# An AFNO block pair on one core: a tile's low half moved ahead of a Newton chain, and the next image's statistics one tile pair behind instead of two

## What is computed

```python
residual = x
h = layer_norm(x, n1_g, n1_b)
h = afno_filter(h, w1, b1, w2, b2)      # rfft2, block MLP with relu and softshrink, irfft2, + its input
h = h + residual
residual = h
h = layer_norm(h, n2_g, n2_b)
h = jax.nn.gelu(h @ mw1 + mb1, approximate=False)
h = h @ mw2 + mb2
return h + residual
```

## Time and profile before

| what | value |
|---|---|
| median of 3 runs | 1695.14 us (1693.17 to 1696.4) |
| the profiled execution, time | 1697.64 us |
| its span, first to last instruction | 1695.9 us |
| PE busy | 1611.5 us, 95% of the span |
| VectorE, ScalarE, GpSimd busy | 1136.1, 949.7, 628.3 us (67, 56, 37%) |
| mean granted clock of TensorE | 0.996 |

### The profile page before, as it was taken

One profiled execution on the slowest core, in us unless ns is written; L12 is line 12 of the kernel. 1 busy time (PEld: TensorE's weight loads), 2 busy tenths in 40 slices (PEclk: granted clock), 3 DMA queues, 4 the chain that ended last, 5 costly groups with the idle time before them and its releaser, 6 DMA issues.

```text
span 1695.9 us, 35295 instructions
## 1 busy us (share of the span) xinstructions
PE 1611.5 (95%) x11336; PEld 1458.9 (86%) x11336; DVE 1136.1 (67%) x2879; ACT 949.7 (56%) x1774; POOL 628.3 (37%) x792
## 2 busy tenths in 40 slices
PE   0799999999999999999999999999999999999999
PEld 0799978888999988888889998888889998788888
DVE  7979576666649856666666976666664795665563
ACT  3655366666535546666634644666663563666665
POOL 3900037776710005777760000777774000111111
PEclk9999999999999999999999999999999999999999
DMA  8400613333300062333320024333332006011111
GB/s 215 180 26 1 227 43 99 105 99 105 101 32 1 13 226 77 110 93 103 108 88 1 1 94 138 94 100 111 105 101 69 2 1 207 14 38 31 37 31 50
DMA packets 166369, 138.86 MB, mean 82 GB/s; under 512 B 9218, under 2 KB 129284, under 8 KB 166276
## 3 DMA queue, kind: packets, MB, share of 16 engines
q1 hardware_dynamic: 165988, 137.15, 25.4%
q10 hardware_dynamic: 288, 0.46, 0.1%
HBM read 70.47 MB, written 67.11 MB: 81 GB/s over the span
## 4 chain that ended last, share of the span: by engine, by line
PE 88%; DVE 4%; POOL 2%; ACT 2%; issue 1%; DMA 0%; DVEq 0%; ACTq 0%
PE ps L692 27%; PE ps L683 7%; PE ps L685 7%; PE ps L639 7%; PE ps L684 7%; PE ps L578 7%; PE ps L534 6%; PE ps L524 5%; PE ps L549 3%; PE ps L672 3%; PE ps L551 3%; PE ps L658 3%; PE ps L664 3%; POOL first L1273 1%; POOL xout L1269 1%; DVE stats L943 1%
## 5 line engine op out<-in xcount | busy, mean ns | idle before, releaser
L692 PEld LDWEIGHTS ps<-mw,gel 128*128 128x128 f32 x4096 | 533.2, 191 | 43.3
L692 PE MATMUL ps<-mw,gel 128*128 128x128 f32 x4096 | 536.4, 274 | 0.0
L803 ACT ACTIVATE gel<-ps,mb1f 128x512 f32<-128x512 f32 x512 | 351.7, 687 | 266.6 <-PE ps L685 235.6
L1314 POOL TENSOR_TENSOR arena<-arena,mb2rep 128x512 f32<-128x512 f32 x128 | 163.8, 1281 | 796.4 <-ACT hn L789 796.4
L683 PE MATMUL ps<-hth,mw1h 128*128 128x512 f32 x512 | 259.9, 508 | 7.5 <-DVE htl L1111 6.5
L1307 POOL TENSOR_SCALAR arena<-xnext,rstd,shift 128x128 f32<-128x128 f32 x384 | 168.8, 463 | 219.4 <-DVE shift L1238 219.4
L789 ACT ACTIVATE hn<-arena,shift,rstd 128x128 f32 (+1 forms) x512 | 221.5, 482 | 24.2 <-DVE shift L1238 23.9
L1094 DVE TENSOR_TENSOR arena<-ps,arena 128x512 f32 (+1 forms) x60 | 41.4, 691 | 259.6 <-PE ps L664 240.9
L685 PE MATMUL ps<-hth,mw1l 128*128 128x512 f32 x512 | 202.1, 395 | 0.0
L684 PE MATMUL ps<-htl,mw1h 128*128 128x512 f32 x512 | 200.9, 392 | 0.0
L774 ACT ACTIVATE osb<-usb,vectors 128x512 f32<-128x512 f32 (+1 forms) x136 | 95.7, 704 | 121.1 <-DVE usb L1002 121.1
(11 more groups left out here) (101 smaller groups left out, 2434.8 us busy)
## 6 DMA issues: line engine op xcount, KB each, us to landing
arena<-aside SPq DMA_DIRECT2D x128, 256.0 KB, 4.8
aside<-gz SPq DMA_DIRECT2D x96, 256.0 KB, 2.9
between<-xout SPq DMA_DIRECT2D x62, 256.0 KB, 2.3
xnext<-between SPq DMA_DIRECT2D x62, 256.0 KB, 3.0
out_dram<-xout SPq DMA_DIRECT2D x62, 256.0 KB, 2.3
aside<-first SPq DMA_DIRECT2D x32, 256.0 KB, 2.3
xnext<-in_x_dram SPq DMA_DIRECT2D x31, 256.0 KB, 3.0
mw1raw<-in_L_mw_dram SPq DMA_DIRECT2D x4, 256.0 KB, 2.5
```

The costliest lines, as they stand in the source:

```text
L692: mm = pe.matmul(ps[:, r % 2, P * i:P * i + P], gel[:, r % 2, m, P * i:P * i + P], mw2[:, m, :], start=(m == 0 and i == 0), stop=(m == CHU ...
L803: act.activation(gel[:, r % 2, m, :], ps[:, 2 + m % 2], ACT.Gelu, bias=mb1f[:, m:m + 1]).then_inc(gelu_out, 1)
L1314: pool.tensor_tensor(t, t, b, ALU.add).then_inc(mb2_done, 1)
```

## The change

Two things are changed, by code written in another order.

First, at the start of the MLP stage, the second tile: TensorE transposes it after the first chunk of `fc1` instead of the second, ScalarE casts it before gelu 1 instead of gelu 2, and VectorE forms its low half before the second Newton chain instead of behind it.

Second, from pair 4 on, pair q handles the next image's pair q - 1. To get there, an additional chain for the next image's pair 2 stands alone behind pair 3 (`nearer`), with a third set of statistics buffers, and only one chain is left behind pair 15. GpSimd no longer adds the biases of tiles 0 and 1 first: bias n now stands behind `z_rows` and `scaled` of the next image's tile n. The last step has no next image; there only the first part of the change acts.

```diff
+NEAR = 3
@@
                 for m in range(CHUNKS):
                     fc1(s, 0, 0, m)
+                    if m == 0:
+                        turn(s, 1, 1)
                     if m == 1:
                         pe.wait_ge(mlp_b, s + 1)
-                        turn(s, 1, 1)
@@
                 for m in range(CHUNKS):
-                    if m == 2:
+                    if m == 1:
                         hi(s, 1, 1)
                     gelu(s, 0, 0, m)
@@
-                    nxt = not last and known >= LAG
+                    nxt = not last and LAG <= known <= PAIRS
+                    near = known > NEAR
@@
-                    if nxt and known >= 4:
-
-                        dve.wait_ge(z_new, TILES * s + 2 * q - 6)
+                    if nxt and near:
+
+                        dve.wait_ge(z_new, TILES * s + 2 * q - 4)
                     if nxt:
                         for e in range(2):
-
-                            dve.wait_ge(xn_in[2 * h + e], 16 * (TILES // 4 * s + i))
+                            r = 2 * (1 - h if near else h) + e
+                            dve.wait_ge(xn_in[r], 16 * (TILES // 4 * s + i + (h if near else 0)))
...
-                            ins = bn(xnext[:, 2 * h + e], 0, stats[:, h, rows_, :])
+                            ins = bn(xnext[:, r], 0, stats[:, h, rows_, :])
+                    if known == 1:
+                        lower(s, 1, 1)
@@
                 pair(1, 1)
+                if not last:
+                    nearer()
@@
-                for n in range(TILES):
-                    j, r = n // 4 - 1, n % 4
-                    if j >= 0 and not last:
-                        ready(j, r)
-                        z_rows(j, r)
-                        scaled(j, r)
-                    if n >= 2:
-                        biased(n - 2)
-                    if j >= 0 and not last:
-                        added(j, r)
+                for n in range(TILES - 4):
+                    ready(n // 4, n % 4)
+                    z_rows(n // 4, n % 4)
+                    scaled(n // 4, n % 4)
                     biased(n)
+                    added(n // 4, n % 4)
```

More of the change, by code:

```diff
@@ L213, in afno @@
         mb1f = sb("mb1f", [P, CHUNKS])
-        stats = sb("stats", [P, 2, 4 * ROWS, 3])
-        rstd = sb("rstd", [P, 2, 4 * ROWS])
+        stats = sb("stats", [P, 3, 4 * ROWS, 3])
+        rstd = sb("rstd", [P, 3, 4 * ROWS])
         var = sb("var", [P, 4 * ROWS])
@@ L245, in afno @@
         mb2rep = at("mb2rep", [P, C], o); o += size(mb2rep.shape)
-        shift = at("shift", [P, 2, 4 * ROWS], o); o += size(shift.shape)
+        shift = at("shift", [P, 3, 4 * ROWS], o); o += size(shift.shape)
         assert o <= work_end
@@ L783, in normal @@
                 if part == 0:
-                    act.wait_ge(rs_done, RS * s + 2 * j + r // 2 + 1)
+                    late = s < len(STEPS) - 1 and (not isinstance(j, int) or n // 2 > NEAR)
+                    act.wait_ge(rs_done, RS * s + 2 * j + r // 2 + 1 + late)
                     if not (isinstance(j, int) and n < 2):
@@ L886, in _ @@
                 normal(s, 0, 2, 0)
-                for r in range(4):
-                    tile(0, r)
-                with act.Fori(1, TILES // 4 - 1) as j:
+                for n in range(8):
+                    tile(n // 4, n % 4)
+                with act.Fori(2, TILES // 4 - 1) as j:
                     for r in range(4):
@@ L1215, in pair @@
                         lower(s, 2 * q - 2, (2 * h - 2) % 4)
-                    if 3 <= known <= PAIRS or last and known > PAIRS:
+                    if known >= 3:
                         x_new(s, i + (2 * h - 5) // 4, (2 * h - 5) % 4)
@@ L1221, in pair @@
                             ins = bn(resid_of(s), (4 * i + 2 * h + e) * ROWS, stats[:, h, e * ROWS:(e + 1) * ROWS, :])
[L1222 to L1224 removed]
+                    if nxt and near:
+                        dve.wait_ge(z_new, TILES * s + 2 * q - 4)
                     if nxt:
                         for e in range(2):
[L1228 to L1229 removed]
+                            r = 2 * (1 - h if near else h) + e
+                            dve.wait_ge(xn_in[r], 16 * (TILES // 4 * s + i + (h if near else 0)))
+                            if isinstance(i, int) and 2 * (q - 1) + e == TILES - 1:
                                 dve.wait_ge(row0_in, 16 * (s + 2))
                             rows_ = slice((2 + e) * ROWS, (3 + e) * ROWS)
[L1232 removed]
+                            ins = bn(xnext[:, r], 0, stats[:, h, rows_, :])
+                    if known == 1:
+                        lower(s, 1, 1)
                     if main or nxt:
@@ L1239, in pair, with nearer @@
                                                  ALU.mult, ALU.mult).then_inc(rs_done, 1)
-                    if 1 <= known <= PAIRS:
+                    if 1 < known <= PAIRS:
                         lower(s, 2 * q - 1, (2 * h - 1) % 4)
-                    if known > PAIRS and not last:
-                        x_new(s, i + (2 * h - 5) // 4, (2 * h - 5) % 4)
                     if known >= 2:
                         x_new(s, i + (2 * h - 4) // 4, 2 * h)
+                def nearer():
+                    for e in range(2):
+                        dve.wait_ge(xn_in[e], 16 * (TILES // 4 * s + 2))
+                        ins = bn(xnext[:, e], 0, stats[:, 2, (2 + e) * ROWS:(3 + e) * ROWS, :])
+                    own.add(ins)
+                    own.settle()
+                    a, b = 2 * ROWS, 4 * ROWS
+                    inverse_std(dve, own, stats[:, 2, a:b, 2], var[:, a:b], rstd[:, 2, a:b], nt0[:, a:b])
+                    dve.scalar_tensor_tensor(shift[:, 2, a:b], stats[:, 2, a:b, 1], -1.0, rstd[:, 2, a:b],
+                                             ALU.mult, ALU.mult).then_inc(rs_done, 1)
                 pair(0, 0)
@@ L1302, in z_rows @@
                 def z_rows(j, r):
+                    p = 2 * j + r // 2
+                    h = p % 2 if p < 2 else 2 if p == 2 else (p + 1) % 2
                     h0 = ROWS * tile_of(j, r)
@@ L1306, in z_rows @@
                         row = (2 + r % 2) * ROWS + k
-                        ins = pool.tensor_scalar(zrow(s + 1, h0 + k), pairs(xnext[:, r, k, :]), rstd[:, r // 2, row:row + 1],
-                                                 shift[:, r // 2, row:row + 1], ALU.mult, ALU.add)
+                        ins = pool.tensor_scalar(zrow(s + 1, h0 + k), pairs(xnext[:, r, k, :]), rstd[:, h, row:row + 1],
+                                                 shift[:, h, row:row + 1], ALU.mult, ALU.add)
                     ins.then_inc(z_new, 1)
@@ L1336, in biased @@
                     bias(s, n // 4, n % 4)
-                for n in range(TILES):
-                    j, r = n // 4 - 1, n % 4
-                    if j >= 0 and not last:
-                        ready(j, r)
-                        z_rows(j, r)
-                        scaled(j, r)
-                    if n >= 2:
-                        biased(n - 2)
-                    if j >= 0 and not last:
-                        added(j, r)
-                j = TILES // 4 - 1
[L1349 to L1353, removed]
-                    biased(n)
[L1355 to L1363, removed]
+                if last:
+                    for n in range(TILES):
+                        biased(n)
+                    continue
+                j = TILES // 4 - 1
+                for n in range(TILES - 4):
+                    ready(n // 4, n % 4)
+                    z_rows(n // 4, n % 4)
+                    scaled(n // 4, n % 4)
+                    biased(n)
+                    added(n // 4, n % 4)
+                for r in (0, 2):
+                    ready(j, r)
+                    z_rows(j, r)
+                    z_rows(j, r + 1)
+                    biased(4 * j + r)
+                    biased(4 * j + r + 1)
+                scaled(j, 0)
+                for r in range(4):
+                    if r < 3:
+                        scaled(j, r + 1)
+                    added(j, r)
     return nc
```

## The result

The changed kernel takes **1733.32 us** (median of 4 executions, 1728.54 to 1735.71) beside 1694.16 us before: ratio 1.0228, 95% interval 1.0208 to 1.0248. It is 39 us slower; 1732 was forecast. Its profiled execution took 1734.34 us, its span is 1732.6 us, its mean granted clock 0.990.

A forecast was written before the change was run, and what follows sets the result against it. TensorE, 88% of the chain of work, was taken as the bound; 14.15 us in each of steps 0 to 2, -1.25 in step 3 and -4.6 at step 2's start gave +36.6: median 1732 us, range 1702 to 1748.

The forecast's parts named there:

- The start of step 2: VectorE's 6.20 us shrink to some 2.5; TensorE's 2.89 us wait and 1.7 us of low clock go: -4.6.
- The first two waits for `x_new`: `fc2` of tiles 2 and 4, steps 0 to 2: late biases delay `x_new`, +1.4 and +2.0 us.
- `nearer`: Extra VectorE chain behind pair 3, steps 0 to 2: blocked beside GpSimd, ends about 673.4; TensorE waits 3.7 us.
- The prediction's stand: Extra chain on VectorE: stands from 667.8 until GpSimd is idle at 671.5, ending about 673.4.
- the strict turn: Blocked chains: one VectorE instruction passes between GpSimd's each time; about 0.6 us less per chain, 3 to 4 in all.
- Pair 4's chain: Steps 0 to 2: stands until GpSimd is idle, ends near 687.0; `fc1` of tile 7 is 4.2 us later.
- The clock: TensorE, steps 0 to 2: lower granted clock after the 4.2 us wait, about 1.7 us charged once a step.
- Steady pairs: Pairs 5 to 16: late loads make about 0.2 us of new wait per chain, 2.4 us a step.
- Part 1: Start of MLP stage, all four steps: tile 1's earlier low half gains 1.25 us a step, 5.0 us in all.
- (a): Rival: the extra chain and pair 4's slip through beside GpSimd; +11.4, median 1706.5 us; chance 0.20.
- (b): Rival, faster: VectorE's idle time before each `h2` covers late biases, loads and extra chain; 1685.5 us; chance 0.09.
- (c): Rival: loads leaving while the store is under way land 0.5 us later, +18, 1750 us; chance 0.08.

The follow-up runs named there:

- experiment 4: Changed kernel with GpSimd's biases as early as before: 0 and 1 first, 2 to 5 behind the z rows of tiles 0 to 3; 1718.76 us.
- experiment 6: Changed kernel with GpSimd forming the next image's residual of tiles 2 to 5 by one-input instructions, not the reference's residual; 1721.53 us.
- experiment 7: Changed kernel with GpSimd's biases early and, in SyncE's queue, the next image's load ahead of the store; 1701.65 us.
- experiment 5: Changed kernel with the next image's load ahead of the store in SyncE's queue; 1720.75 us.
- experiment 9: Kernel before with the build of the new layer's spectral weights three slots later at the start of step 2; 1692.68 us.
- part 1 alone: Kernel before with only tile 1's low half ahead of the second Newton chain; 1694.24 us, and 1693.46 us in a second series.
- experiment 8: Changed kernel with early biases, load ahead of the store, and one-input residual instructions for tiles 2 to 5 (not the reference's); 1689.8 us.
- the later build: Spectral weights' build three slots later at step 2's start; added to the kernel before with tile 1's earlier low half: 1689.1 and 1693.1 us.

## Why the prediction was right, and where it was not

The span was forecast at 1732.5 us and is 1732.6, which flatters the sum. The mechanisms it named for the loss are the ones found, but several of its terms are off and cancel, and that part of the agreement is luck. The MLP stages of steps 0 to 2 came to 40.1 us instead of 42.5. The start of step 2 gave -4.7 and step 3's MLP stage -1.4, much as forecast. The stages ahead of the MLP, for which the sum had no term, brought +2.7 in all and filled the gap.

- **The first two waits for `x_new`**: 1.4 and 2.0 forecast, 1.36 and 1.76 measured in step 1, and experiment 4 removes them. Delay after the second 2.08 (686.02 - 20.48 - 663.46), forecast 2.15.
- **`nearer`**: forecast to start at 665.5 and end at 673.4; it started at 685.88 - 20.48 = 665.4 and ended at 693.22 - 20.48 = 672.74. Its wait is 2.75 us and the delay grew by 3.1, not 3.7. The step that failed is the manner: the chain did not stand until GpSimd was idle, one of its instructions passed at each of GpSimd's. So no single one took the 2 to 4 us that the prediction wanted to see. That is the rule of the Trainium skill ("SBUF — State Buffer", "Who interferes with whom") that the prediction weighed and set aside for the earlier trace rows; the traces of after and of experiments 6 and 7 agree with it for GpSimd's two-input instructions, at 1.14 to 1.27 us for each held one. The chain took 5.9 us, 3.4 over a free one of 2.5. The prediction's stand made that 4.0, and the strict turn that it set aside, 0.6 less, would have met it.
- **Pair 4's chain**: with the clock, the delay behind it was forecast at 11.75 and was 8.69. The term of 4.2 had a wrong cause. Only two instructions were held (1.15 and 1.20, 2.0 us more than free); the other 1.78 is the late load, which the prediction charged only from pair 5 on. Each of the two costs something by itself. VectorE's two low halves, of tiles 6 and 7, are 10.28 us apart in after, 8.07 in experiment 7 (load in time, two instructions held) and 8.45 in experiment 4 (load late by 1.68, chain nearly free), where TensorE at full clock needs 6.78. In both experiments no wait is seen in front of tile 7, because the low clock behind the wait for tile 6 has taken that time already.
- **The clock**: 1.7 a step was charged behind the second wait. In step 1 it fell behind the first, the 2.75 us in front of tile 6:

```profile
697.00:700.00 3.00, 3.00 (x12) 2.77 (x13) 2.30 (x7) 1.45 (x3) 3.00 (x5) 0.53 0.45 127
700.00:705.00 5.00, 5.00 (x35) 4.49 (x35) 3.71 (x8) 2.32 (x4) 4.37 (x5) 0.94 0.23 81
```

  that is 3 x 0.47 + 5 x 0.06 = 1.7 us, most of it at the lower level of 1.2 GHz; the size was right, the place not. The wait that followed, 1.63 us, is smaller by what the slow clock had already cost. In step 0 it fell behind the second wait, as forecast, to 0.85 over 20 us (285 to 305), 3.0 us. With a wait of 3.44 instead of 1.63 us in front of tile 7, and without part 1's 1.3, that stage is the dearest, 16.25.
- **Steady pairs**: 0.2 us a pair forecast, 0.24 measured; experiment 5 shows it to be the load.
- **Start of step 2**: -4.6 forecast, -4.7 measured, and experiment 9 shows that the build's meeting with GpSimd was the cause. The filter behind it was 3.1 us shorter too, which no term held; part 2 need not be its cause, for in both executions of part 1 alone it was 3.8 shorter. All that lies ahead of the MLP stage was longer by 2.75, 1.48 and 1.49 us in the steps 0, 1 and 3.
- **Part 1**: mis-sized, and most so in the net. Step 1's reading was taken for all four steps. The prediction's own row speaks against that: 6.5 us in 8 waits cannot hold four of 1.56 and four of 0.38. Step 0's was 0.31, and step 0 gave 0.16; the others gave some 1.45 each. And of some 4 us gained by waits the clock left none that can be measured.

Of the rivals, (a), chains not held up, fell with the rows above and with experiment 6; (b), cover by VectorE's idle time, with the `x_new` waits; (c), dearer loads, with the pitch. For the version of experiment 8, (b)'s mechanism is true: once the loads and biases come early and nothing blocks the chains, VectorE's idle time covers the rest.

## What to carry to other kernels

Before a consumer is moved one step nearer to its producer, look at everything in between that was hidden by the old distance: here a load queued behind a store and a bias queued behind other work cost as much as the moved chain itself, and each of the two went with one change of order. A chain of short dependent VectorE instructions does not belong beside two-input instructions of GpSimd: a chain of 2.5 us became 5.9 and 8.5, and its one-input instructions were held as well (1.15 to 1.20 us). And where a gain of waits is below 0.5%, compare the mean clock of the executions too: it can take the gain back even where the waits have gone.

## What was not expected of the hardware

A GpSimd instruction with one input did not hold VectorE up in the way of one with two: beside a plain scaled copy of 128x512 (1.49 us) chain instructions kept 0.17 us but for one of 0.61, beside z rows they took 0.38 to 0.40, beside two-input ones 1.14 to 1.27. Part 1 alone, a kernel with fewer waits, ran at a lower mean clock, 0.995 instead of 0.997 to 0.998, in two series on two chips; with the later build added it did so in one series of two. Why in the earlier trace rows two instructions stood until the last of five of GpSimd's had ended, and in the earlier trace rows one through two, while elsewhere one passed at each, was not tried and stays open.
